# Feed-forward, attention and feed-forward of one layer written as one block

## The reference, cut to what matters

```python
x = x + 0.5 * _L0_ffn_ref(_layernorm(x), ...)    # softmax router over 8 experts, rank-8 LoRA, base matmul
x = x + _L0_attn_ref(_layernorm(x), ...)         # 16 heads of 8 channels, causal, T5 relative bias, softmax
x = x + 0.5 * _L0_ffn_ref(_layernorm(x), ...)    # the same weights once more
x = x + 0.5 * _L1_ffn_ref(_layernorm(x), ...)    # mixture of 16 experts, then retention, then experts again
```

## Time and profile before

| | |
|---|---|
| runs | 1361.97, 1363.6, 1371.08 us; median 1363.6 |
| profiled execution | 1358.9 us, its span 1357.1 us, mean granted TensorE clock 0.968 |
| ffn1 | 0 to 55.2 us |
| attention | 55.6 to 332.1 us (first scores at 66.8) |
| ffn2 | 332.5 to 384.2 us |
| experts, retention, experts | 386 to 1357 us |
| busy share of the span | PE 92%, DVE 71%, ACT 56%, POOL 57% |

### The profile page before, as it was taken

How to read it: one execution, slowest core, us unless ns; L and a number is a source line. 1 busy time by engine, 2 the same in 40 slices (tenths; PEclk the granted TensorE clock), 3 DMA queues, 4 the chain that set the end, 5 groups by cost and what they waited for, 6 DMA issues and landing times. The chain is left out here.

```text
span 1357.1 us, 34817 instructions
## 1 busy us (share of the span) xinstructions
PE 1254.3 (92%) x10236; PEld 1065.9 (79%) x10236; DVE 966.3 (71%) x4102; ACT 766.5 (56%) x1805; POOL 767.3 (57%) x1010
## 2 busy tenths in 40 slices
PE   7799999997868889999869999999999979999998
PEld 5667777775746678888759999998988867888887
DVE  6578888875868655656448788888889857555654
ACT  2268888885365334444326766766667654344443
POOL 2178888885352755555325656566677554345543
PEclk9889999999779989999979999999999999999999
DMA  5399920001230112221112212111222112112221
GB/s 149 96 272 273 270 84 0 0 2 44 72 117 16 64 34 29 30 30 30 15 47 56 50 49 51 50 50 48 51 61 56 33 37 79 37 28 32 30 30 15
DMA packets 102887, 85.27 MB, mean 63 GB/s; under 512 B 10791, under 2 KB 90505, under 8 KB 102490
## 3 DMA queue, kind: packets, MB, share of 16 engines
q1 hardware_dynamic: 84084, 65.51, 17.5%
q0 software_dynamic: 17280, 16.17, 6.9%
q10 hardware_dynamic: 1382, 1.83, 0.5%
HBM read 20.92 MB, written 45.78 MB: 49 GB/s over the span
## 5 line engine op out<-in xcount | busy, mean ns | idle before, releaser
L1984 POOL TENSOR_TENSOR attn_z<-attn_top,attn_z 128x256 f32<-128x256 f32 x256 | 154.7, 615 | 35.1 <-DVE attn_top L1935 34.5
L1935 DVE CUSTOM_DVE_ANT_0 attn_z<-banks,rel_bias 128x128 f32<-128x128 f32 (+1 forms) x512 | 147.5, 354 | 25.1 <-PE banks L2065 23.7
L2408 POOL TENSOR_TENSOR ret_rotated<-ret_twins 128x512 f32<-128x512 f32 x64 | 82.2, 1284 | 132.3 <-DVE ret_twins L2318 132.2
L2016 ACT ACTIVATE attn_prob<-banks 128x384 f32<-128x384 f32 x256 | 111.9, 489 | 24.1 <-PE banks L2075 17.5
L1005 DVE SCALAR_TENSOR_TENSOR moe_block_act<-banks,moe_block_weights,moe_block_gated 128x128 f32<-128x128 f32 x276 | 77.7, 344 | 64.3 <-ACT moe_block_gated L1060 39.8
L1550 DVE SCALAR_TENSOR_TENSOR moe_block_act<-banks,moe_block_weights,moe_block_gated 128x128 f32<-128x128 f32 x276 | 77.8, 344 | 62.9 <-ACT moe_block_gated L1644 39.2
L2471 ACT ACTIVATE ret_normed<-banks,ret_head_shift,ret_head_rstd 128x128 f32<-128x128 f32 x256 | 96.5, 458 | 45.5 <-DVE ret_head_shift L2342 45.2
L2075 PE MATMUL banks<-ident,attn_z 128*128 128x128 f32 x768 | 112.4, 282 | 0.6
L2075 PEld LDWEIGHTS banks<-ident,attn_z 128*128 128x128 f32 x768 | 83.6, 142 | 20.6 <-issue 14.6
L2503 PE MATMUL banks<-ret_x_hi,ret_hi 128*128 128x256 f32 x256 | 84.8, 331 | 1.9 <-ACT ret_gate L2464 1.0
L1597 POOL DMA_INDIRECT out<-moe_block_y,moe_taken x37 | 58.5, 1581 | 46.4 <-ACT moe_block_y L1654 34.1
(11 more groups left out here) (359 smaller groups left out, 4039.0 us busy)
## 6 DMA issues: line engine op xcount, KB each, us to landing
slots<-moe_pad SPq DMA_DIRECT2D x12, 2560.0 KB, 23.5
ret_twins<-ret_twins SPq DMA_DIRECT2D x256, 64.0 KB, 2.0
moe_stage<-in_moe_w SPq DMA_DIRECT2D x4, 576.0 KB, 6.8
bias_reversed<-scratch SPq DMA_DIRECT2D x1, 2048.0 KB, 9.7
y_rows<-moe_pad SPq DMA_DIRECT2D x1, 2048.0 KB, 8.8
back_of_seq<-y_rows SPq DMA_DIRECT2D x16, 128.0 KB, 2.4
out<-x_res SPq DMA_DIRECT2D x8, 256.0 KB, 2.5
ret_stage<-in_ret_w SPq DMA_DIRECT2D x16, 96.0 KB, 2.1
```

The lines of the kernel that those rows point to most:

```text
L1935: last = dve.tensor_tensor_reduce(out=z[:, s, cols], in0=ps_s[:, i, cols], in1=bias, scale=1.0, scalar=-3.0e38, op0=ALU.add, op1=ALU.max, ...
L1984: pool.tensor_tensor(z[:, s, P:WIDTH], top[:, s, 1:2].to_broadcast([P, WIDTH - P]), z[:, s, P:WIDTH], ALU.subtract).then_inc(shifted1, 1)
L2016: act.activation(prob[:, slot(k, i), :], ps_p[:, i % 2, 0:WIDTH], ACT.Exp, scale=-1.0).then_inc(prob_ready, 1)
L2408: pool.tensor_tensor(rotated[:, k % 2], twins[:, k % 2, 0], twins[:, k % 2, 1], ALU.add).then_inc(rotated_ready, 1)
```

## The change

The three phases become one block. The feed-forward code is a class `FfnStage` used twice, the attention a class `Attention`; each has `vector`, `gpsimd`, `tensor` and `scalar`, which emit what stands ahead of the pipeline and return a `Steps` object that can emit one step (`at`) or a loop. `front_phase` calls these four for each engine and then `in_order`, which sets the same order on all engines:

- ffn1's steps as before, and behind step 1 the attention's steps -14 and -13, behind step 2 steps -12 to -9, behind steps 3, 4 and 5 one each (-8, -7, -6);
- the attention's steps -5 to -1, then its loop, then the straight steps from 48;
- behind steps 57, 59, 60, 61 and 62 of the attention ffn2's steps -4, -3, -2, -1 and 0, then ffn2's steps 1 to 7.

Barriers become semaphores: a sequence's layernorm waits for its group's residual in ffn1 (`group_done`), the first scores wait for all eight of them, ffn2's layernorm waits for the attention's residuals, and ffn2's first transposes wait for the last `biased_done`. The feed-forward's PSUM layout moves: `ps_y` from banks 5 and 6 to 4 and 5, `ps_o` from two banks to one. Only flips 0 to 3 stay in ffn1's steps 0 to 3. Flips 4, 5 and 6, 7 stand behind the attention's steps -5 and -4. The memsets of `v_aug` stand at the start of DVE's queue. `Attention.gpsimd` begins with a wait for `attn_loaded`. On SP `load_attention`, `fill_slots` and `load_moe` follow each other with nothing between them, so the slots are filled from when `moe_pad` has landed.

```diff
-def software_pipeline(engine, iterations, units, stages):
...
+class Steps:
+
+    def __init__(self, engine, iterations, units, stages):
+        self.engine, self.last, self.units, self.stages = engine, iterations * units, units, stages
+
+    def at(self, step):
+        for lead, emit in self.stages:
+            if 0 <= step + lead < self.last:
+                emit((step + lead) // self.units, (step + lead) % self.units)
+
+    def loop(self, iterations):
+        with self.engine.Fori(0, iterations) as it:
+            for step in range(self.units):
+                for lead, emit in self.stages:
+                    emit(it + (step + lead) // self.units, (step + lead) % self.units)
...
-FLIPS = 8
+FLIPS, FFN_FLIPS = 8, 4
...
+        self.ps_t, self.ps_y = banks[:, 0:2, :], banks[:, 4:6, :]
+        self.ps_small = banks[:, 2, 0:GROUP * 16].rearrange("p (j e) -> p j e", e=16)
+        self.ps_o = banks[0:LORA_ROWS + 1, 3, :]
...
-                if x_first is not None:
-                    dve.wait_ge(x_first if isinstance(it, int) and it * U + u < FIRST_GROUPS else x_rest, 16)
+                dve.wait_ge(*group_ready(it * U + u))
...
+            return Steps(dve, GROUPS // U, U, [(3, normalise), (2, router_shift), (4, layernorm), (2, gates), (0, residual)])
+
+        def gpsimd(pool):
...
-                wait_free(pe, omT_ready, count(it, u, 2))
+                wait_free(pe, omT_ready, count(it, u, 1))
                 for j in range(GROUP):
-                    last = pe.transpose(ps_o[:, u % 2, j * P:(j + 1) * P], om[:, u % 2, j, :], ident[:, :])
+                    last = pe.transpose(ps_o[:, j * P:(j + 1) * P], om[:, u % 2, j, :], ident[:, :])
...
+            return Steps(pe, GROUPS // U, U, [(3, transpose_x), (1, transpose_om)] + in_step(lambda n: opening.flip(pe, n), 0, FFN_FLIPS)
+                         + [(3, router_and_mid), (1, project)])
...
+                dve.wait_ge(group_done, it + 1)
...
+                if isinstance(it, int) and it == 0 and k < HEAD_GROUPS and i % 2 == 0:
+                    dve.wait_ge(opening.flip_copied, h // 2 + 1)
...
+            pool.wait_ge(opening.attn_loaded, len(ATTENTION_LOADS) * 16)
...
+                if isinstance(it, int) and it * U + k == 0:
+                    pe.wait_ge(group_done, GROUPS)
...
+                if isinstance(it, int) and it * U + k == 0:
+                    pe.wait_ge(opening.flip_copied, FLIPS)
...
+LEAD_IN = {1: (-14, -13), 2: (-12, -11, -10, -9), 3: (-8,), 4: (-7,), 5: (-6,)}
+LATE_FLIPS = {-5: (4, 5), -4: (6, 7)}
+LOOPS, LAST_QUADS = 6, 62
+BESIDE = {57: -4, 59: -3, 60: -2, 61: -1, 62: 0}
...
+        def in_order(ffn1, quads, ffn2, late_flip, before_second):
+            for n in range(-4, GROUPS):
+                ffn1.at(n)
+                for step in LEAD_IN.get(n, ()):
+                    quads.at(step)
+            for step in range(-5, 0):
+                quads.at(step)
+                for flip in LATE_FLIPS.get(step, ()):
+                    late_flip(flip)
+            quads.loop(LOOPS)
+            for step in range(LOOPS * quads.units, LAST_QUADS + 1):
+                quads.at(step)
+                if step in BESIDE:
+                    before_second(BESIDE[step])
+                    ffn2.at(BESIDE[step])
+            for n in range(1, GROUPS):
+                ffn2.at(n)
...
+            def scores_read(n):
+                if n == -3:
+                    pe.wait_ge(attention.biased_done, BATCHES * HEADS)
+
+            in_order(first.tensor(pe), attention.tensor(pe), second.tensor(pe), lambda n: opening.flip(pe, n), scores_read)
...
+            def background(sync):
+                load_attention(sync)
+                fill_slots(sync)
+                load_moe(sync)
...
+            buffers = FfnBuffers(nc, front_ctx, banks)
+            first = FfnStage(nc, "ffn1", used, buffers, x_res, ident, neg_half, lora,
+                             lambda g: (x_first if g < FIRST_GROUPS else x_rest, 16), opening=opening)
+            attention = Attention(nc, front_ctx, "attn", banks, used, x_res, ident, neg_half, attn, opening, first.x_updated)
+            second = FfnStage(nc, "ffn2", used, buffers, x_res, ident, neg_half, lora,
+                              lambda g: (attention.x_updated, 2 * g + 2), split=(split_on_scalar, split_on_pool, MOE_PARTS))
+            front_phase(nc, banks, used, x_res, first, attention, second, opening, background)
```

More of the change, by code:

```diff
@@ L26 @@
 LORA_SCALING = 2.0
-def software_pipeline(engine, iterations, units, stages):
-    most = max(lead for lead, _ in stages)
-    ahead = -(-most // units)
-    for step in range(-most, 0):
-        for lead, emit in stages:
-            if step + lead >= 0:
-                emit((step + lead) // units, (step + lead) % units)
-    if iterations > ahead:
-        with engine.Fori(0, iterations - ahead) as it:
-            for step in range(units):
-                for lead, emit in stages:
-                    emit(it + (step + lead) // units, (step + lead) % units)
-    for step in range((iterations - ahead) * units, iterations * units):
-        for lead, emit in stages:
-            if step + lead < iterations * units:
-                emit((step + lead) // units, (step + lead) % units)
+class Steps:
[10 more added lines that the diff above has]
+                    emit(it + (step + lead) // self.units, (step + lead) % self.units)
 def new_sem(nc, used, name):
@@ L1791, with __init__ @@
 MASKED = -1.0e30
-def attention_phase(nc, tag, banks, used, x_res, ident, neg_half, w, background):
-    GU = 2
-    U = GU * HEAD_GROUPS
-    Z, PR = 8, 8
-    with ExitStack() as ctx:
+class Attention:
+    def __init__(self, nc, ctx, tag, banks, used, x_res, ident, neg_half, w, opening, group_done):
+        GU = 2
+        U = GU * HEAD_GROUPS
+        Z, PR = 8, 8
         def sb(name, shape, dt=F32):
@@ L2755, in fill_slots, with load_moe @@
                         sync.dma_start(of_blocks[:, lo:hi, :], moe_pad[:, :].unsqueeze(1).to_broadcast([P, hi - lo, ROW])).then_inc(slots_filled[i], 16)
[L2757 to L2767 removed]
+            def load_moe(sync):
                 for dst, name in moe_loads:
```

162 lines of the change are left out of this document (80 added, 82 removed).

## The result

| | median of the runs, us | least to most | runs | ratio to before, with its interval |
|---|---|---|---|---|
| before | 1362.1 | 1359.3 to 1371.1 | 20 | |
| changed | 1369.2 | 1363.7 to 1381.8 | 20 | 1.0057, 1.0033 to 1.0081 |

The change makes the kernel slower by 7 us, 0.57%. The time lies inside the forecast's range, but the kernel moved the other way, and by more than the interval.

A forecast was written before the change was run, and what follows sets the result against it. It took PE as busy nearly everywhere, DVE and PE both near full in ffn1, with latency between phases. Terms 7.9 + 7.4 - 12.3 + 1.6 - 5.5 = -0.9 gave a median of 1362.7 us, range 1354.5 to 1370.5.

The forecast's parts named there:

- A: Head of ffn1: POOL's first inverse_std now waits for attn_loaded, nothing hides it; +7.9 us, bounds 7.5 and 8.4.
- B: The attention's lead-in inside ffn1's steps 1 to 5; +7.4 us, bounds 4.6 and 12.
- PE trails DVE by some 1 us: In ffn1: PE's lag behind DVE, used to price step 3's add_v_bias at 2.2 us.
- C: Boundary from ffn1 to attention: first scores follow the last residual by 0.1 us instead of 12.4; -12.3 us.
- D: Attention's quads 0 to 4: full clock from the start, but four late flips added; +1.6 us, bounds -1.8 and +4.
- E: Attention's end: four steps joined with ffn2's first steps bring residual 1 earlier; -5.5 us, bounds -9 and -1.
- The rest of the program keeps its length: Claim that everything outside the five priced places stays as long as before; 0 us.
- Rival 2: TensorE loses its clock in ffn1, decisive if the fall comes in step 3 or later; +5.1 us, 1368.7, chance 0.2.
- Rivals 1, 3 and 4: Interleaving cheaper, 1355.3 (chance 0.25); POOL's wait free, 1354.8 (0.03); earlier slot fill delays ffn1, +5 or more (0.04).

The follow-up runs named there:

- warm_lead: Changed kernel plus filler matmuls on PE ahead of the transposes in ffn1's steps 2, 3 and 4; ratio to before 1.0016.
- again: The changed kernel unaltered, run and profiled a second time; 1367.5 us, ratio to before 1.0037.
- lead_behind: Changed kernel with the attention's steps -14 to -6 all behind ffn1's last step, without the barrier; 1369.6 us, ratio to before 1.0050.
- best3: Changed kernel with POOL's wait later, all flips in ffn1, first statistics and ffn2's step -4 one step earlier, fillers in ffn1 and ffn2; 1345.5 us, 0.9876.
- warm_both: Changed kernel with fillers in ffn1's steps 2 to 4 and ahead of ffn2's transposes of groups 0, 1 and 3; ratio to before 1.0012.
- warm_all: Changed kernel with filler matmuls on PE in ffn1 and in the whole tail; 1363.7 us, ratio to before 0.9993.
- fills_flips: Changed kernel in its own order, POOL's wait included, with all eight flips in ffn1 and fillers in ffn1 and ffn2; 1354.4 us, 0.9932.

## Why the prediction was right or wrong

**A was right**: 7.6 to 7.8 us against 7.9, the wait ended by `bias_flip`'s landing, and the rest of ffn1 shifted by it.

**B was wrong, as the term that was mis-sized**: 7.4 forecast, 12.2 and 18.3 measured. The parts in DVE's steps were right (7.17 us for steps with an insertion, POOL's wait of 1.22 twice). The step that failed is "PE trails DVE by some 1 us", with zero net for steps 4 and 5: both rest on PE's durations at full clock. `warm_lead` shows the term at full clock, 7.9; the other 4 to 10 us are half clock. In `again`, whose span is 8.5 us above the forecast, B is 4.8 of them, E 3.6, residual 1 to 7 another 1.7 and the rest of the program 0.8, less 1.6 for D and 0.6 for the loop. Its upper bound of 12, which named this cause, was itself too low: I let a step at half clock last 8.5 us and did not let a second fall follow the first, nor `project_v` and `project_qk` double while DVE stood behind them.

**C was right**: 0.05 to 0.06 us from the residual to the scores. But the forecast called it a gain of the order. `lead_behind`, with the lead-in where it was, has its first scores no later than any profile of the changed kernel: B and C together, 12.2 - 12.3 and 18.3 - 12.3, gained nothing or cost 6. At full clock they gain 4.4 (7.9 - 12.3, `warm_lead`).

**D**: +1.6 forecast with "clock 1.00 between", and measured 0.0 at full clock with the late flips in place (`again`, `warm_lead`), +3.7 where the clock was at half (the changed kernel's profile), -1.7 with the flips back in ffn1, and -2.6 where the clock stayed full as well (`best3`), so the lower bound of -1.8 was too high. The steps of 4.4 and 6.9 came as 3.9 and 5.8.

**E was right in its mechanism and wrong in its size**: -5.5 forecast, -3.1 and -1.9 measured, -6.4 at full clock. The joint steps 61 and 62 were priced with PE at full clock, although the same stretch of before ran at half (0.50 from 334 to 352 us), as the forecast says itself beside its upper bound of -1, "cold clock kept throughout". The measured values lie between the sum and that bound.

**"The rest of the program keeps its length"** was wrong inside ffn2: residual 1 to 7 takes 25.6, 27.2 or 31.1 us, by where the clock falls behind the gap of group 7, where PE stands idle for 1.8 to 2.7 us (2.28 in before, 1.77 in the changed kernel, 2.69 in `warm_both`). Behind ffn2 the program took 0.8 and 3.5 us longer.

**Rival 2**, TensorE loses its clock in ffn1, is what happened, down to its condition: the fall comes in step 3, behind an idle time of 2.33 us. It gave 1368.7; the median is 1369.2. That match is partly luck, since its B is too small and the later stretches are missing. The evidence stood in my text, a third of each step idle on PE and a fall at 374 behind a pause, and I gave it 0.2 against the sum without it. The Trainium skill, "TensorE: Matmul & The Clock Gate", Part 1, says that idling halves the clock and sustained work restores it; the trace agrees (0.50 at 52 to 54 behind the idle 2.33 us, 1.00 in the loop), but how soon full work restores it differs from place to place: after some 7 us at 52 to 59, and not for 20 us in `warm_all`, where PE was busy for 18.00 of 18 us at 0.50. Rivals 1, 3 and 4 fell: nothing was cheaper, the wait cost 7.6, and the DMA share of 0.97 stands beside a full clock in `warm_lead`.

Put shortly, the forecast is near the full-clock sum. With D and B as `warm_lead` has them and E as `fills_flips` has it, it is 7.9 + 7.9 - 12.3 + 0.0 - 6.4 = -2.9 against the profile of before. `fills_flips` itself was measured 5.7 below that profile: its flips in ffn1 make 1.0 of the difference, the loop and ffn2's later steps 1.5. The real kernel runs its gaps at half clock.

What stays open: why one execution loses the clock behind a gap behind which another with the same ffn1 keeps it (1.74 and 1.75 us in `warm_lead` and `warm_all`); what moves the time behind ffn2 by 0 to 4 us; and what the order alone is worth at full clock. The split of the 8.9 us between POOL's wait and the two other moves is worked out from positions, not measured by itself.

## What to carry to other kernels

A step moved into a phase whose engine was just busy enough can cost twice: its own waits, and TensorE's clock behind the gap that it opens. Price every PE duration behind a new gap at both levels, ask whether PE leads there, and read the profile's clock column over the stretch that is being rearranged. Where such a gap can't be closed with work, matmuls into the bank that PE overwrites next hold the clock (0.54% here for the kernel before, nothing else changed); but a fall that they don't prevent makes each of them about twice as long (2.67 us for three in `warm_both` instead of 1.46), and then they stand in the way of real work.
